# The feed-forward's last product as two passes over rounded parts, in a fused two-layer transformer kernel

## The reference, cut to what matters

```python
SCALE = 1.0 / 127.0
wg = w_gate.astype(x.dtype) * SCALE      # w_gate, w_up: 384 x 128 integers from -127 to 127
wu = w_up.astype(x.dtype) * SCALE
wd = w_down.astype(x.dtype) * SCALE      # w_down: 128 x 384 integers from -127 to 127
gate = jnp.einsum('bsd,hd->bsh', x, wg)
up = jnp.einsum('bsd,hd->bsh', x, wu)
h = jax.nn.silu(gate) * up
return jnp.einsum('bsh,dh->bsd', h, wd)
...
x = x + attn_a(layernorm(x)); x = x + ffn(layernorm(x))
x = x + attn_b(layernorm(x)); x = x + ffn(layernorm(x))
```

## Time and profile before

| | |
|---|---|
| median of 3 | 648.86 us |
| profiled execution | 643.88 us |
| its span | 640.5 us |
| PE busy | 590.4 us, 92% |
| PE weight loads busy | 443.4 us, 69% |
| DVE busy | 488.8 us, 76% |
| ACT busy | 425.6 us, 66% |
| POOL busy | 389.5 us, 61% |
| chain that ended last | PE 66%, DVE 10%, issue 8%, POOL 5%, ACT 5% |
| its largest lines | L1477 13%, L1455 8%, L1431 8%, L1408 7% |

### The profile page before, as it was taken

How to read it: one execution, slowest core, us unless ns; L and a number is a source line. 1 busy time by engine, 2 the same in 40 slices (tenths; PEclk the granted TensorE clock), 3 DMA queues, 4 the chain that set the end, 5 groups by cost and what they waited for, 6 DMA issues and landing times.

```text
span 640.5 us, 18862 instructions
## 1 busy us (share of the span) xinstructions
PE 590.4 (92%) x6534; PEld 443.4 (69%) x6534; DVE 488.8 (76%) x1421; ACT 425.6 (66%) x1057; POOL 389.5 (61%) x824
## 2 busy tenths in 40 slices
PE   2579989999999999999899999999999999999993
PEld 2245546777766767766677788788888888888763
DVE  2388868888888888987677887887888888888423
ACT  2014756777787777787677677677776776676871
POOL 5755555666777666666676665577666666663322
PEclk9676999999999999999899999999999999999998
DMA  3587656665566644454544543343444534440000
GB/s 98 125 255 166 158 138 149 147 159 147 138 159 163 150 122 121 126 135 124 123 129 106 133 107 99 94 108 97 125 98 108 119 101 112 121 109 24 19 11 20
DMA packets 74383, 75.90 MB, mean 118 GB/s; under 512 B 10988, under 2 KB 68908, under 8 KB 69676
## 3 DMA queue, kind: packets, MB, share of 16 engines
q1 hardware_dynamic: 74284, 74.64, 46.7%
HBM read 46.86 MB, written 23.33 MB: 110 GB/s over the span
## 4 chain that ended last, share of the span: by engine, by line
PE 66%; DVE 10%; issue 8%; POOL 5%; ACT 5%; DMA 3%; SPq 2%; ACTq 0%; POOLq 0%; DVEq 0%
PE banks L1477 13%; PE banks L1455 8%; PE banks L1431 8%; PE banks L1408 7%; PE banks L1347 6%; PE banks L1434 3%; PE banks L1399 3%; PE banks L1400 2%; DVE top L1078 2%; PE banks L1440 2%; PE banks L1379 2%; ACT probs_t L1267 2%; PE banks L1438 2%; PE banks L1436 2%; PE banks L1458 2%
## 5 line engine op out<-in xcount | busy, mean ns | idle before, releaser
L1267 ACT ACTIVATE probs_t<-banks 128x512 f32<-128x512 f32 (+1 forms) x512 | 276.5, 551 | 104.8 <-PE banks L1455 55.2
L1072 DVE TENSOR_REDUCE neg_shift<-banks 128x2 f32<-128x512 f32 x256 | 167.0, 681 | 33.8 <-PE banks L1431 31.0
L1477 PE MATMUL banks<-probs_t,v_ext 128*32 128x256 f32 (+1 forms) x2048 | 124.1, 360 | 0.0
L1431 PE MATMUL banks<-k_stack,q_stack 72*128 72x256 bf16 x512 | 103.5, 287 | 17.8 <-DMA k_stack<-k_image 6.3
L1077 DVE MAX8 top<-banks 128x8 f32<-128x128 f32 x256 | 74.5, 291 | 43.6 <-PE banks L1440 41.8
L1078 DVE MAX8 top<-banks 128x8 f32<-128x256 f32 x256 | 106.2, 415 | 0.0
L1455 PE MATMUL banks<-q_stack,k_stack 75*128 75x256 bf16 x512 | 99.6, 276 | 0.6 <-DMA q_stack<-neg_shift_rows 0.5
L963 POOL TENSOR_TENSOR hidden<-up_tanh,gate_half 128x256 f32<-128x256 f32 x96 | 69.5, 727 | 42.9 <-DVE up_tanh L1118 42.0
L1431 PEld LDWEIGHTS banks<-k_stack,q_stack 72*128 72x128 bf16 x512 | 41.8, 100 | 62.0 <-DVE neg_shift L1072 36.5
L1477 PEld LDWEIGHTS banks<-probs_t,v_ext 128*32 128x32 f32 x2048 | 53.6, 109 | 43.6 <-issue 12.5
L1434 PE MATMUL banks<-k_stack,q_stack 123*128 123x128 bf16 x256 | 57.1, 223 | 7.6 <-DVE top L1078 3.3
(11 more groups left out here) (106 smaller groups left out, 1334.1 us busy)
## 6 DMA issues: line engine op xcount, KB each, us to landing
q_stack<-q_image SPq DMA_DIRECT2D x96, 192.0 KB
k_stack<-k_image SPq DMA_DIRECT2D x96, 192.0 KB
q_image<-qk_parts SPq DMA_DIRECT2D x32, 192.0 KB, 2.3
k_image<-qk_parts SPq DMA_DIRECT2D x32, 192.0 KB, 2.4
q_image<-qk_parts SPq DMA_DIRECT2D x32, 128.0 KB, 2.2
o_image<-out_t SPq DMA_DIRECT2D x32, 128.0 KB, 2.4
out_compact<-o_image SPq DMA_DIRECT2D x64, 32.0 KB, 1.9
rdenominators<-r_image SPq DMA_DIRECT2D x16, 128.0 KB, 2.4
```

Source lines behind the costliest of these rows:

```text
L1072: dve.tensor_reduce(m.nm[:, n % STACKS, h, :], scores.rearrange("p (q k) -> p q k", q=TT), AX.X, ALU.max, negate=True).then_inc(reduced, 1)
L1267: act.activation(m.pt[:, g % 2, i, 0:size], shifted_banks[:, j % 2, 0:size], ACT.Exp if is_soft(n) else ACT.Relu, scale=SCALE if is_soft(n ...
L1431: ins = pe.matmul(scores[:, qt * T:(qt + 1) * T], qs[0:STACK, h, qt * P:(qt + 1) * P], ks[0:STACK, h, :], start=True, stop=True)
L1477: ins = pe.matmul(out_bank[32 * i:32 * i + 32, at + skip:at + T], v_windows(v, kt)[:, Q * g + i, :], m.pt[:, g % 2, i, kt * T:(kt + 1) * T ...
```

## The change

- `down` takes its input in two float32r parts, `hidden_high` and `hidden_low`, and its weights as unscaled integers in float32r. Six fp32 matmuls (12 records) become 12 float32r matmuls of the same 128x128 weights and 128 columns.
- POOL's product goes back into `up_tanh`. ACT rounds it into `hidden_high` (`high{c}`), POOL subtracts that from the product into `hidden_low` (`low{c}`). That is 96 instructions more on ACT and 96 more on POOL. An `up_tanh` buffer is released after `low`, not after the product.
- One conversion of all weights takes the place of two; the scale moves into `gate_half`.
- The table of offsets is changed.

The diff, without the general program and without the declarations of semaphores:

```diff
-    m.wf = sb("wf", [P, 3 * HIDDEN])
-    m.w_gate_up = sb("w_gate_up", [P, 2 * HIDDEN], F32R)
+    m.w_ffn = sb("w_ffn", [P, 3 * HIDDEN], F32R)
...
-    m.hid = sb("hidden", [P, NC_H, T])
+    m.hid_high = sb("hidden_high", [P, NC_H, T], F32R)
+    m.hid_low = sb("hidden_low", [P, NC_H, T], F32R)
...
-          cos_q=-21, sin_q=-21, cos_k=-18, sin_k=-18, take_v=-13,
+          cos_q=-21, sin_q=-20, cos_k=-18, sin_k=-18, take_v=-13,
           split_q=-18, split_k=-16, store_q=-15, store_k=-12, load_q=-12, load_k=-8,
-          tau=16, shift_split_soft=17, shift_split_plain=18, excess=20, shift=24, load_shift=24,
-          pass2=29, pv=36, take_out=49, store_out=50, load_out=53, invert=57, store_rden=57, load_rden=60,
-          xb=64, normalise=65, proj=71, residual=72, f_bn=72, f_aggr=73, f_rstd=75, f_norm=76,
-          fxT=78, gu0=82, gu1=84, gu2=86, up0=83, up1=84, up2=86, hid0=85, hid1=87, hid2=88,
-          down=90, f_residual=92, store_x=92)
+          tau=16, shift_split_soft=17, shift_split_plain=17, excess=20, shift=23, load_shift=23,
+          pass2=29, pv=36, take_out=49, store_out=50, load_out=53, invert=57, store_rden=57, load_rden=61,
+          xb=65, normalise=65, proj=71, residual=72, f_bn=72, f_aggr=73, f_rstd=75, f_norm=78,
+          fxT=79, gu0=82, gu1=84, gu2=86, up0=83, up1=84, up2=86, hid0=85, hid1=87, hid2=88,
+          high0=85, high1=88, high2=89, low0=87, low1=88, low2=90, down=94, f_residual=94, store_x=95)
...
             def hidden(n, c):
                 wait_freed(pool, f"gu{c}", n)
-                if n > 0:
-                    wait_filled(pool, "down", n - 1)
                 k = (n * NC_H + c) % 3
-                pool.tensor_tensor(m.hid[:, c, :], m.t1[:, k, :], m.g05[:, k, :], ALU.mult).then_inc(hid_ready, 1)
+                pool.tensor_tensor(m.t1[:, k, :], m.t1[:, k, :], m.g05[:, k, :], ALU.mult).then_inc(hid_product, 1)
+
+            def hidden_low(n, c):
+                turn = n * NC_H + c
+                pool.wait_ge(hid_high, turn + 1)
+                pool.tensor_tensor(m.hid_low[:, c, :], m.t1[:, turn % 3, :], m.hid_high[:, c, :].bitcast(F32),
+                                   ALU.subtract)\
+                    .then_inc(hid_ready, 1)
...
-                dve.tensor_copy(m.w_gate_up[:, :], m.wf_int[:, 0:2 * HIDDEN]).then_inc(dequantised, 1)
-                dve.tensor_scalar(m.wf[:, :], m.wf_int[:, :], W_SCALE, None, ALU.mult).then_inc(dequantised, 1)
+                dve.tensor_copy(m.w_ffn[:, :], m.wf_int[:, :]).then_inc(converted, 1)
...
+            def hidden_high(n, c):
+                turn = n * NC_H + c
+                act.wait_ge(hid_product, turn + 1)
+                if n > 0:
+                    wait_filled(act, "down", n - 1)
+                act.copy(m.hid_high[:, c, :], m.t1[:, turn % 3, :]).then_inc(hid_high, 1)
...
+                parts = (m.hid_high, m.hid_low)
                 for tt in range(TT):
                     for c in range(NC_H):
-                        ins = pe.matmul(bank("down", n)[:, tt * D:(tt + 1) * D], m.hid[:, c, tt * P:(tt + 1) * P],
-                                        down_w[:, c * D:(c + 1) * D], start=(c == 0), stop=(c == NC_H - 1))
+                        for s, part in enumerate(parts):
+                            ins = pe.matmul(bank("down", n)[:, tt * D:(tt + 1) * D], part[:, c, tt * P:(tt + 1) * P],
+                                            down_w[:, c * D:(c + 1) * D], start=(c == 0 and s == 0),
+                                            stop=(c == NC_H - 1 and s == 1))
                 fills(ins, "down", n)
```

More of the change, by code:

```diff
@@ L192 @@
 AT = dict(a_bn=-29, a_aggr=-28, a_rstd=-27, a_norm=-25, xT=-23, q=-21, k=-18, v=-16,
-          cos_q=-21, sin_q=-21, cos_k=-18, sin_k=-18, take_v=-13,
+          cos_q=-21, sin_q=-20, cos_k=-18, sin_k=-18, take_v=-13,
           split_q=-18, split_k=-16, store_q=-15, store_k=-12, load_q=-12, load_k=-8,
-          tau=16, shift_split_soft=17, shift_split_plain=18, excess=20, shift=24, load_shift=24,
-          pass2=29, pv=36, take_out=49, store_out=50, load_out=53, invert=57, store_rden=57, load_rden=60,
-          xb=64, normalise=65, proj=71, residual=72, f_bn=72, f_aggr=73, f_rstd=75, f_norm=76,
-          fxT=78, gu0=82, gu1=84, gu2=86, up0=83, up1=84, up2=86, hid0=85, hid1=87, hid2=88,
-          down=90, f_residual=92, store_x=92)
+          tau=16, shift_split_soft=17, shift_split_plain=17, excess=20, shift=23, load_shift=23,
[3 more added lines that the diff above has]
+          high0=85, high1=88, high2=89, low0=87, low1=88, low2=90, down=94, f_residual=94, store_x=95)
 LATE = ("xb", "proj", "residual", "f_bn", "f_aggr", "f_rstd", "f_norm", "fxT", "gu0", "gu1", "gu2", "up0", "up1", "up2",
-        "hid0", "hid1", "hid2", "down", "f_residual", "store_x")
+        "hid0", "hid1", "hid2", "high0", "high1", "high2", "low0", "low1", "low2", "down", "f_residual", "store_x")
 SECOND = dict(a_bn=-17, a_aggr=-17, a_rstd=-17, a_norm=-16, xT=-15, q=-14, cos_q=-14, sin_q=-14,
@@ L321, in general_programs @@
     gate_up_bank = m.banks[:, 6, :]
-    gate_w, up_w, down_w = (m.wf[:, n * HIDDEN:(n + 1) * HIDDEN] for n in range(3))
+    gate_w, up_w, down_w = (m.w_ffn[:, n * HIDDEN:(n + 1) * HIDDEN].bitcast(F32) for n in range(3))
     w, at = m.wb, WB
@@ L708, in main_phase @@
     out_bank = m.banks[:, 4, :]
-    gate_w, up_w = (m.w_gate_up[:, n * HIDDEN:(n + 1) * HIDDEN] for n in range(2))
-    down_w = m.wf[:, 2 * HIDDEN:3 * HIDDEN]
+    gate_w, up_w, down_w = (m.w_ffn[:, n * HIDDEN:(n + 1) * HIDDEN] for n in range(3))
     place = number_dense_uses()
@@ L992, in _ @@
                         hidden(n, c)
+                for c in range(NC_H):
+                    if (n := due(step, f"low{c}")) is not None:
+                        hidden_low(n, c)
                 if (n := due(step, "a_rstd")) is not None:
@@ L1310, in _ @@
                         gate(n, c)
+                for c in range(NC_H):
+                    if (n := due(step, f"high{c}")) is not None:
+                        hidden_high(n, c)
                 if (n := due(step, "a_norm")) is not None:
```

17 lines of the change are left out of this document (10 added, 7 removed).

## The result

The changed kernel takes 660.85 us (median of 4 executions) against 644.69 us of the kernel before (4): ratio 1.027, 95% interval 1.014 to 1.039. Run again later beside other variants it took 657.69 us (10 executions) against 650.92 us (13): ratio 1.018, interval 1.013 to 1.022. So it is slower, by about 2%.

The account below looks back on a forecast made before the run. PE was taken as the bound wherever it has no hole. Terms +2.6 + 4 - 4 + 4 = +6.6 us gave 650.5 on the profiled 643.9, 655.5 by the median; forecast 653 us between them, range 632 to 670.

Parts of the forecast that it names:

- within 2%: Whole kernel: time within 2% of the kernel before, chance 0.62, against 0.18 for faster and 0.20 for slower.
- Twelve passes, +2.6 us: `down` on PE: twelve float32r matmuls at 0.12 us, paced by weight loads, 1.44 us an item; +2.6 us over 32 items.
- Float32r loads as bf16 does: Rival at `down`: 128 columns cost 0.06 us, `down` halves, 20 us go; 628 by profile, 633 by median; chance 0.16.
- The added work on POOL and ACT, +4 us beside soft heads: Beside soft heads: both engines have room, but the order of ACT's roundings costs 0.3 us in each of 13 items; +4 us.
- ACT waits for POOL: Rival beside soft heads: POOL's first product comes after ACT reaches `high0`, and PE stops; 667 us by profile; chance 0.17.
- The moved stages, -4 us in 17 items: Beside plain heads, items 13 to 29: `down` in slot 14 fills PE's hole, a third of 0.74 us an item; -4 us.
- The end, +4 us: Items 30 and 31: added subtractions make item 31's chain 1.7 us later, the exchange with ACT another 2.2; together +4 us.
- The start: At the kernel's start: DVE has one conversion less, counted at nothing.

Follow-up runs that it names:

- Six loads: Changed kernel, but beside plain heads integer weights stay stationary and 256 columns stream: six matmuls, not twelve, output transposed; 652.09 us, ratio 1.007 to the kernel before.
- bf16 parts: Changed kernel with both parts and the integer weights of `down` in bf16, holding fewer bits; 647.95 us, ratio 1.004 to the kernel before.
- new offsets alone: Kernel before, its fp32 one-product arithmetic kept, with only the changed table of offsets; 647.43 us against 648.46, ratio 0.999.

## Why the prediction was right or wrong

The time was forecast at 653 us in a range of 632 to 670 and came to 661 and 658. The median of before stood at 645 to 651 in the runs beside it. What I called likeliest, within 2%, held for neither measurement clearly: 2.7% and 1.8%, intervals across 2%. Several terms were off, and one was missing. That both times lie in the range is in part luck: its upper end stood for ACT waiting beside soft heads, and the time went elsewhere. In the first profile the terms came to 0 us beside soft heads, -2.4 beside plain heads, +7.0 at the end, and +10.1 in a stretch for which the sum had no term.

*Twelve passes, +2.6 us.* It was 32 x -0.05 = -1.6 us. The reason held: twelve loads, each 190 to 200 ns long in the records, pace `down`. "Six loads" and "bf16 parts" show it from both sides (0.75 us for six loads, 0.67 us for twelve bf16 loads). The rival *Float32r loads as bf16 does* fell by the same rows, and its price was wrong as well: it let 20 us go with a `down` of half the time, "since PE is the bound". "bf16 parts" had that `down`, and gained about half of that: 9.7 us by the medians, 12.9 and 9.4 by the spans of the changed kernel's two profiles. Only 1.9 us of it come from item 24 on and 1.4 or 4.1 beside soft heads; 6.7 or 2.5 come at items 22 and 23, and 2.6 or 2.9 at the end. In the steady stretches PE was the last to end, but little was gained by making it faster (0.18 of 0.58 us in "six loads"), so others must have been close behind. The Trainium skill, "TensorE: Matmul & The Clock Gate", section "Weight-path perf modes", leaves open on which side of its FP32 rule float32r stands; by these runs it is on FP32's side.

*The added work on POOL and ACT, +4 us beside soft heads.* An item there takes 18.10 us against 18.06, and the 11 items from 5 to 16 take 200.0 us in the first profile of either kernel. But the second profile of the changed kernel has +2.7 us there, and all seven with float32r parts in these items average +2.0 (0.0 to +3.2), against 0.0 and +0.9 in the two with the arithmetic of before. So the term was between nothing and some 2 us; with 3 us of scatter between profiles it isn't told more closely. ACT waited for POOL's product 11.2 us in all 96 roundings, and a wait of over 10 us was what I had set as the sign of the rival *ACT waits for POOL*. It was that mechanism, but in another place: there are only 13 such waits in the whole run, the longest is the one in item 22 (2.46 us), and none is on the list between 120 and 280 us. POOL's wait at `f_rstd` went from 62.3 to 5.9 us: the subtractions did fill that hole.

*The moved stages, -4 us in 17 items.* Beside plain heads the gain was 0.43 us for a steady item, more than the 0.25 taken. But the 17 items were miscounted: only items 24 to 31 are steady, and over the stretch the whole gain is 2.4 us. What I didn't see is that the stages of items 16 to 18 slide by four steps an item. There the new offsets cost 2.9 us and, with the exchange, 3.0 to 7.2 us more. **This is the step that failed: I costed the change on the two steady patterns and named the stretch between them without working it out.** The order in which POOL meets the threshold wait, the product and the splits there could have been read from both orders beforehand, and the 1.52 us for which POOL waited for `neg_shift` at that place before would have been the row for it.

*The end, +4 us.* It was 7.0. The two `down` come 3.0 + 2.0 = 5.0 us later, and I had 1.7 + 2.2 = 3.9. The exchange in series was a right cause: 3.6 of the 5.0 us came back with one product in items 30 and 31, and the other 1.4 stay unexplained. The remaining 1.9 us, which the sum did not have, are `down` below the full clock: twelve float32r matmuls at the 1.2 GHz level take 2.8 us. That the last `down` of before had taken 2.03 us and not 1.38 was the sign of it.

*The start.* +3.5 us in the first profile is not shown to be the change's: kernels with the new offsets show -0.3 to +4.0 there, among them "new offsets alone", with the old arithmetic, +2.7.

## What to carry to other kernels

Where a table slides stages against each other, work out the stretch in which they slide; the steady pattern says nothing of it. Here an exchange between two engines cost little where both had holes, and most where one of them had a wait of its own ahead of its half, and at the end, where nothing covered it: the old form can be kept for just those items. A chain that lies on PE throughout bounds what a slower PE costs, not what a faster one brings: of 0.6 us saved in each item, 0.18 arrived beside plain heads and about 0.25 beside soft ones. And before a difference of a few microseconds in one stretch is put down to an edit, compare two profiles of the same kernel: here they differed by 2.7 us beside soft heads and by 4.2 at items 22 and 23.

## What the runs showed of the hardware

- A float32r matmul with 128x128 weights costs about 0.11 us with 128 columns (twelve in 1.29 to 1.33) and 0.125 with 256 (six in 0.75), and its load record lasts as long as an fp32 one (200 ns over the whole run with its half-clock end, 193 before). With bf16 on both sides the pace is 0.67 / 12 = 0.056 us and the record 100 ns.
- With bf16 parts ACT's rounding takes 411 ns against 409, and POOL's subtraction 676 against 731.
- After a stop of PE (1.68 us of waiting, then 0.51 us some 25 us later) the granted clock was 0.83 and 0.73 over 10 us in one profile of the changed kernel, and stayed at 1.00 in another with the same stops. The two differ by 4.2 us in that stretch.
- SyncE took 0.31 to 0.80 us for each of 18 DMAs issued one after the other, 10.9 us of an item's 18.
